# Preparing the next batch's operands in another order in a cross-attention kernel

## The chip, the cores and the metric

The kernel runs on one core of one Trainium2 chip. Its time is the device time of one execution in microseconds, the median of several runs. A core has five engines that each work through a queue of their own in program order: TensorE (PE), VectorE (DVE), ScalarE (ACT), GpSimd (POOL) and SyncE (SP, which issues DMAs here). They wait for each other by semaphores only.

## The reference

For each of 16 batches: x is 112 x 320, the context 375 x 512, of which the last 4 rows are the "ip" rows and the first 371 the text. There are 20 heads of 16 channels.

```python
q = heads(x @ W_q); k_t = heads(text @ W_k); v_t = heads(text @ W_v)
probs_t = softmax(q k_t^T / 4)                       # 112 x 371 per head
text_out = probs_t v_t
qsem = l2norm(probs_t text)                          # 112 x 512 per head
sem  = qsem · l2norm(ip)                             # 112 x 4
probs_ip = softmax(q k_ip^T / 4 + 0.5 * sem) * mask
out = (text_out + probs_ip v_ip) @ W_out + b_out + x
```

The kernel never forms `probs_t text`. It uses the Gram matrix G = text text^T (371 x 371): the squared norm of a row p of `probs_t text` is the quadratic form p G p^T, and its products with the ip rows are four more columns beside the values.

## The kernel before, in words

**Numbers.** Each float32 operand is split into a high and a low float16 part, and products are made as hi·hi + hi·lo + lo·hi. ScalarE writes the high parts out of PSUM, VectorE the low parts (value minus high part).

**Heads and steps.** The outer loop runs over 16 batches, the inner one over 20 heads; one pass of the inner loop is a step (`body` in each engine's program). In step h TensorE issues, in this order: `scores(h+3)` (one matmul, L535), `transposes(h+1)` of the probabilities (three float32 transposes, L543), in some steps one part of `finish` of the batch before, `products(h)` (p times G, L561 and L562, and p times the values, L569 and L571), and then half of a piece of the next batch's preparation (`make`). VectorE in step h: `minimum(h+3)` (L892), `probs_lo(h+1)` (`pT_lo`, L897), the low part of a piece (`make_lo`), a part of `finish`, and the quadratic form `quadratic(h)` (L907). ScalarE: `probs_hi(h+1)` (L734), `make_hi`, `exps(h+3)`, `halve(h+1)` (L740). GpSimd: `duals(h+1)` (L397: the low half of the probabilities, SBUF to SBUF), and small things.

**Pieces.** The next batch's operands come in ten pieces, which share two PSUM banks by turns (`ps_prep[k % 2]`). Piece 0 is Q, 1 to 3 are K, three are value blocks (V: 125 context rows times W_v, with 12 matmuls of 320 columns) and three are row blocks of the Gram matrix (G). Only the upper triangle of G is made: block 0 has 375 columns, block 1 250, block 2 125. So gram block 0 is the longest piece and block 2 the shortest. Block 2's piece also transposes the three upper blocks (L510) to fill the lower triangle, so it needs the high parts of blocks 0 and 1. `MAKE_STEP` makes piece k in steps 2k-1 and 2k, half each; `TAKE_STEP` evicts it to SBUF in step 2k+1 (L695 to L717 on ScalarE, L855 to L886 on VectorE). Evicting a V piece is one instruction on each engine (L716, L884). Evicting a G piece is three on ScalarE (L708, L710, L711) and four on VectorE (L871, L873, L874, L880; the profile shows them under their helpers' lines, L832 and L835).

**The end of a batch.** The ip softmax of the batch before is a chain of 13 small VectorE instructions (`soft`, numbers 0 to 12). `SOFT_AT` says in which step and at which of three places they are issued: place 0 is ahead of `probs_lo`, place 1 behind the eviction, place 2 behind `quadratic`. Between numbers 9 and 10 ScalarE takes an exponential, in step `EXP_STEP`, as its last work of the step. Number 12 is `fprob` (L968); TensorE transposes it in `finish(0)` (L594) in step 12. The four parts of `finish` use the pieces' banks, in steps 12, 14, 16 and 18; each waits until all pieces evicted so far are out of their banks:

```python
            def finish(f, k, made):
                bank = ps_prep[(k + 1) % 2]
                pe.wait_ge(s_prep_lo, made)          # made: all pieces up to h // 2 - 1
                reached(pe, s_fin_ev, NF * f.n + k)
                if k == 0:
                    pe.wait_ge(s_soft, SOFT * (f.n + 1))
```

The last batch prepares nothing; its `soft` and `finish` are one step later. The start-up makes the pieces of batch 0 one after the other in three banks, with the same order of pieces.

Of the kernel before, what the change touches and what calls it, by code (L numbers as in the profile page):

```python
# [15 lines left out]
H = 20  # L16
# [18 lines left out]


NM = 10
PIECE_Q, PIECES_K, PIECES_V, PIECES_G = 0, (1, 2, 3), (5, 7, 9), (4, 6, 8)
PIECE_TURN_G = PIECES_G[-1]
TURNED_G = 160  # L40
G_DIAG = 384
# [12 lines left out]
LAST_FINISH_STEP = {13: 0, 15: 1, 17: 2, 19: 3}  # L54


VALS_STEP, POW_STEPS, EXP_STEP = 0, (3, 4, 5, 6), 9

SOFT_AT = {(2, 0): 0, (2, 1): 1, (2, 2): 2, (3, 0): 3,
           (7, 2): 4, (8, 0): 5, (8, 1): 6, (8, 2): 7, (9, 0): 8, (9, 1): 9,  # L60
           (10, 1): 10, (10, 2): 11, (11, 0): 12}
SOFT_LATER = 1
SOFT = len(SOFT_AT)
SOFT_NORMS, SOFT_ARGS = 4, 10
# [9 lines left out]
def channels(j):  # L74
    return P if j < CC - 1 else CR
# [15 lines left out]
def build(nc, x, x_t, ctx_t, ip, ip_t, mask, w_q, w_k, w_v, w_k_ip, w_v_ip, w_out, b_out, out):  # L91
    scratch = nc.dram_tensor("v_ip_scratch", (B * NIP, C), F32, kind="Internal").ap()
    stack = ExitStack()
    with stack:
# [126 lines left out]
        def reached(eng, s, value):  # L221

            if not (isinstance(value, int) and value <= 0):
                eng.wait_ge(s, value)
# [233 lines left out]
        def _(pe):  # L458
# [12 lines left out]
            def make(a, k, banks=ps_prep, half0=0, half1=2, at=0):  # L471

                bank = banks[k % len(banks)]
                text = (text_hi[a.odd], text_lo[a.odd])
                part = range(half0 * EC // 2, half1 * EC // 2)
                if half0 == 0:
                    reached(pe, s_prep_lo, NM * a.n + k + 1 - len(banks))
                    reached(pe, s_fin_ev, NF * (a.n - 2) + sum(step <= at for step in FINISH_STEP))
                if k == PIECE_Q:
                    pe.wait_ge(s_split_pool, len(POOL_PIECES) * (a.n + 1))  # L480
                if k == PIECES_K[0]:
                    pe.wait_ge(s_split_lo, len(DVE_PIECES) * (a.n + 1))
                if k == PIECE_TURN_G and half0 == 0:
                    pe.wait_ge(s_prep_hi, NM * a.n + PIECES_G[1] + 1)
                if k in PIECES_K:
                    j = k - PIECES_K[0]
                    m = channels(j)
                    if j < CC - 1:
                        last = split3(bank[:, 0:TX], lambda h_, e: w[h_][:, e, 0, j * P:(j + 1) * P],
                                      lambda h_, e: text[h_][:, e, 0:TX], EC, part)  # L490
                    else:
                        if isinstance(a.n, int) and a.n == 0:
                            pe.wait_ge(s_wk_last, 2)
                        for e in part:
                            nc.tensor.matmul(bank[:, 0:TX], wk_last[:, e, :, :].rearrange("p a c -> p (a c)"), text[0][:, e, 0:TX],  # L495
                                             start=(e == 0), stop=(e == EC - 1), skip_group_check=True)
                            last = nc.tensor.matmul(bank[:, 0:TX], wk_last[:, e, :, :].rearrange("p a c -> p (a c)"), text[1][:, e, 0:TX],  # L497
                                                    start=False, stop=(e == EC - 1), skip_group_check=True)
                elif k == PIECE_Q:
                    for j in range(CC):  # L500
                        last = split3(bank[:, j * S:(j + 1) * S], lambda h_, c: (wq_hi, wq_lo)[h_][:, c, j * P:(j + 1) * P],
                                      lambda h_, c: (x_hi, x_lo)[h_][:, c, :], CC)
                elif k in PIECES_G:
                    i = PIECES_G.index(k)
                    m, n0 = TROWS[i], i * TC
                    hi, lo = text
                    if k == PIECE_TURN_G and half0 == 0:
                        g, blocks = gram_hi[a.odd], bank[:, TURNED_G:G_DIAG].bitcast(F16)
                        for n, (r0, c0) in enumerate(((0, 1), (0, 2), (1, 2))):
                            nc.tensor.transpose(blocks[0:TROWS[c0], n * P:n * P + TC], g[:, r0, c0 * TC:c0 * TC + TROWS[c0]], ident_16[0:TC, 0:TC])  # L510

                    for e in part:
                        nc.tensor.matmul(bank[:, G_DIAG:G_DIAG + m], hi[:, e, n0:n0 + P], lo[:, e, n0:n0 + m],  # L513
                                         start=(e == 0), stop=(e == EC - 1))
                    for e in part:
                        for term, l, r_, c in ((0, hi, hi, 0), (1, hi, lo, m), (2, lo, hi, m)):
                            last = nc.tensor.matmul(bank[:, c:T - n0], l[:, e, n0:n0 + P], r_[:, e, n0 + c:T],  # L517
                                                    start=(e == 0 and term == 0), stop=(e == EC - 1 and term == 2), skip_group_check=True)
                else:
                    i = PIECES_V.index(k)  # L520
                    m, n0 = TROWS[i], i * TC
                    last = split3(bank[:, 0:C], lambda h_, e: text[h_][:, e, n0:n0 + P],
                                  lambda h_, e: w[h_][:, e, 1, :], EC, part)
                if half1 == 2:
                    last.then_inc(s_prep, 1)
# [96 lines left out]
            last.then_inc(s_setup_pe, 1)  # L622
            pe.wait_ge(s_const, 3)
            pe.wait_ge(s_wsplit_lo, 3)
            for k in range(PIECES_G[0], PIECES_G[1] + 1):
                make(start, k, SETUP_BANKS)
            pe.wait_ge(s_w[3], 16)
            for e in range(EC):
                last = nc.tensor.matmul(ps_val[0:64, 0:C], ip_T[:, e, :], w_raw[:, e, 3, :], start=(e == 0), stop=(e == EC - 1))
            last.then_inc(s_setup_pe, 1)  # L630
            for k in range(PIECES_G[1] + 1, NM - 1):
                make(start, k, SETUP_BANKS)
            pe.wait_ge(s_ipdiag, 1)
            pe.wait_ge(s_setup_ev, 2)
# [35 lines left out]
        def _(act):  # L670
# [16 lines left out]
            def make_hi(a, k, banks=ps_prep):  # L687
# [8 lines left out]
                elif k == PIECE_Q:  # L696
                    reached(act, s_qst[1 - a.odd], 256 * (a.last().pair + 1))
                    for e in range(2):
                        last = nc.scalar.activation(q_hi[:, :, e, 0:S], bank[:, 0:CC * S].rearrange("p (c s) -> p c s", s=S),
                                                    ACT.Copy, scale=q_mask[:, e:e + 1])  # L700
                elif k in PIECES_G:
                    i = PIECES_G.index(k)
                    m, n0 = TROWS[i], i * TC
                    if i == 0:
                        reached(act, s_val, H * (a.n - 1))
                    if k == PIECE_TURN_G:
                        nc.scalar.activation(gram_hi[a.odd][:, 1, 0:TC], bank[0:TC, TURNED_G:G_DIAG].bitcast(F16)[:, 0:TC], ACT.Copy)
                    nc.scalar.activation(gram_hi[a.odd][0:m, i, n0:TX], bank[0:m, 0:TX - n0], ACT.Copy, scale=G_DOWN)  # L708
                    if i < NT - 1:
                        nc.scalar.activation(gram_2hi[0:m, i, n0 + m:TX], bank[0:m, m:TX - n0], ACT.Copy, scale=2 * G_DOWN)  # L710
                    last = nc.scalar.activation(val[a.odd][0:m, i, :, DH + 1:VW],  # L711
                                                bank[0:m, TX - n0:T - n0].unsqueeze(1).to_broadcast([m, H, NIP]), ACT.Copy, scale=G_DOWN)
                else:
                    i = PIECES_V.index(k)
                    m = TROWS[i]
                    last = nc.scalar.activation(val[a.odd][0:m, i, :, 0:DH], bank[0:m, 0:C].rearrange("p (h d) -> p h d", d=DH),  # L716
                                                ACT.Copy, scale=1.0 / W_UP)  # L717
                last.then_inc(s_prep_hi, 1)
# [61 lines left out]
            split_weight(w_hi[:, :, 1, :], w_raw[:, :, 1, :], s_w[1], 1)  # L780
            for k in range(NX):
                split_hi(Batch(1, 1, 0), k)
            for k in range(PIECES_G[0], NM - 1):
                make_hi(start, k, SETUP_BANKS)
            exps(start, 0)
            exps(start, 1)
# [43 lines left out]
        def _(dve):  # L830
# [16 lines left out]
            def make_lo(a, k, banks=ps_prep):  # L847
# [15 lines left out]
                        last = low_part(q_lo[:, :, e, 0:S], bank[:, 0:CC * S].rearrange("p (c s) -> p c s", s=S),  # L863
                                        q_mask[:, e:e + 1], q_hi[:, :, e, 0:S])
                elif k in PIECES_G:
                    i = PIECES_G.index(k)
                    m, n0 = TROWS[i], i * TC
                    if i == 0:
                        reached(dve, s_val, H * (a.n - 1))
                    g, gl, v = gram_hi[a.odd], gram_lo[a.odd], val[a.odd]  # L870
                    low_part(gl[0:m, i, n0:n0 + m], bank[0:m, 0:m], G_DOWN, g[0:m, i, n0:n0 + m]).then_inc(s_part_lo, 1)  # L871
                    if i < NT - 1:
# [8 lines left out]
                else:  # L881
                    i = PIECES_V.index(k)
                    m = TROWS[i]
                    last = low_part(val[a.odd][0:m, i, :, VW:VW + DH], bank[0:m, 0:C].rearrange("p (h d) -> p h d", d=DH),  # L884
                                    1.0 / W_UP, val[a.odd][0:m, i, :, 0:DH])
                last.then_inc(s_prep_lo, 1)  # L886
# [141 lines left out]
                                           op0=ALU.mult, op1=ALU.add, accum_out=ip_norm[:, 0:1]).then_inc(s_chain, 1)  # L1028
            dve.wait_ge(s_chain, 2)
            nc.vector.tensor_scalar(ip_norm[:, 1:2], ip_norm[:, 0:1], EPS * EPS, None, ALU.max).then_inc(s_ipsq, 1)  # L1030
            for k in range(PIECES_G[0], PIECES_G[0] + 2):
                make_lo(start, k, SETUP_BANKS)
            dve.wait_ge(s_pool_set, 2)

# [2 lines left out]
            nc.vector.tensor_scalar(ip_diag[:, :], ident[0:64, 0:64], ip_norm[:, 3:4], None, ALU.mult).then_inc(s_ipdiag, 1)  # L1037
            for k in range(NX):
                split_lo(Batch(1, 1, 0), k)
            for k in range(PIECES_G[0] + 2, NM - 1):  # L1040
                make_lo(start, k, SETUP_BANKS)
            dve.wait_ge(s_setup_pe, 2)
            nc.vector.tensor_copy(vip_rows[:, :], ps_val[0:64, 0:C]).then_inc(s_setup_ev, 1)
# [72 lines left out]
```

## Time and profile before

| | us |
|---|---|
| Median of three runs | 788.32 (787.84 to 790.66) |
| The profiled execution | 787.84 |
| its span, first to last instruction | 786.0 |
| TensorE busy, of the span | 749.9 |
| VectorE busy | 661.2 |
| ScalarE busy | 584.0 |
| GpSimd busy | 446.7 |

The profile shows one execution. "Busy" is the time in which an engine had at least one instruction in flight. Matmuls overlap each other, so the distance from one start to the next says more than the length of one. In the rows, times are microseconds from the start of the span.

### The profile page before, as it was taken

The page shows a single profiled execution, that of the slowest core. Times are in us where ns is not written, and L with a number is a line of the kernel's source. Part 1 is how long each engine was busy: PE and PEld are TensorE (multiplying, and loading weights), DVE is VectorE, ACT ScalarE, POOL GpSimd, SP SyncE. Part 2 cuts the span into 40 slices and gives each one's busy share as a digit, 9 for nine tenths or more (in the row PEclk, how much of TensorE's full clock was granted, in tenths as well). Part 3 has the DMA queues.
Part 4 walks back from the last instruction along what each step waited for, and adds up shares of the span by engine and source line. Part 5 has one row for each costly group of instructions (what it writes and reads, how often), then busy time and mean ns, then how long its engine had stood idle before and what let it go on. Part 6 is the DMA issues. An engine that isn't in the chain of part 4 may idle for free.

```text
span 786.0 us, 23798 instructions
## 1 busy us (share of the span) xinstructions
PE 749.9 (95%) x7730; PEld 588.4 (75%) x7730; DVE 661.2 (84%) x1960; ACT 584.0 (74%) x1702; POOL 446.7 (57%) x558
## 2 busy tenths in 40 slices
PE   3889999999999999999999999999999999999983
PEld 2668778787877878787787878778787777878661
DVE  5878898988989898898989889898998989889883
ACT  4378787877878787787878778787877878777770
POOL 4135574656647465664746566474656647464762
PEclk9999999999999999999999999999999999999995
DMA  9323222221412223140222314022231402021000
GB/s 268 92 55 72 79 68 62 61 79 44 103 27 66 65 59 81 42 106 24 68 65 58 81 40 108 23 67 66 55 84 41 106 21 69 21 54 41 9 2 15
DMA packets 71465, 50.02 MB, mean 64 GB/s; under 512 B 16640, under 2 KB 71280, under 8 KB 71344
## 3 DMA queue, kind: packets, MB, share of 16 engines
q1 hardware_dynamic: 68416, 45.14, 22.3%
q10 hardware_dynamic: 2928, 3.36, 1.4%
q8 instruction: 65, 1.06, 0.6%
q14 instruction: 56, 0.46, 0.2%
HBM read 20.80 MB, written 2.38 MB: 29 GB/s over the span
## 4 chain that ended last, share of the span: by engine, by line
PE 91%; issue 2%; DVE 2%; POOL 2%; ACT 1%; DMA 1%; SPq 0%; POOLq 0%; DVEq 0%; ACTq 0%
PE ps_prep L465 22%; PE ps_gram L561 19%; PE ps_pT L543 13%; PE ps_gram L562 12%; PE ps_score L535 6%; PE ps_prep L517 5%; PE ps_val L569 2%; PE ps_val L571 2%; PE ps_prep L513 1%; PE ps_prep L495 1%; PE ps_prep L597 1%; PE ps_prep L497 1%; PE ps_gram L465 1%; DMA xt_sb<-in_x_t 1%; POOL dual L397 1%
## 5 line engine op out<-in xcount | busy, mean ns | idle before, releaser
L397 POOL TENSOR_TENSOR dual<-prob 112x371 f32<-112x371 f32 x320 | 282.9, 884 | 306.6 <-ACT prob L740 287.4
L561 PE MATMUL ps_gram<-gram_hi,pT_hi 125*128 125x371 f16 (+1 forms) x960 | 303.9, 320 | 0.0
L562 PE MATMUL ps_gram<-gram_lo,pT_hi 125*128 125x371 f16 (+2 forms) x960 | 255.9, 267 | 0.0
L734 ACT ACTIVATE pT_hi<-ps_pT 125x336 f16<-125x336 f32 x320 | 144.6, 452 | 143.4 <-PE ps_pT L543 140.0
L724 ACT ACTIVATE prob<-ps_score,low 112x371 f32<-112x371 f32 x320 | 183.9, 575 | 16.5 <-DVE low L892 10.6
L892 DVE TENSOR_REDUCE low<-ps_score 112x1 f32<-112x371 f32 x320 | 171.2, 535 | 28.6 <-PE ps_score L535 24.8
L897 DVE TENSOR_TENSOR pT_lo<-ps_pT,pT_hi 125x336 f16<-125x336 f32 x320 | 160.0, 500 | 38.1 <-ACT pT_hi L734 34.0
L907 DVE CUSTOM_DVE_ANT_0 quad_junk<-ps_gram,dual 112x371 f32<-112x371 f32 x320 | 171.1, 535 | 12.4 <-PE ps_gram L562 6.0
L740 ACT ACTIVATE prob<-prob 112x371 f16<-112x371 f32 x320 | 168.9, 528 | 0.0
L569 PE MATMUL ps_val<-val,pT_hi 125*128 125x42 f16 (+1 forms) x960 | 166.9, 182 | 0.0
L543 PE MATMUL ps_pT<-ident,prob 112*125 112x112 f32 x960 | 157.0, 272 | 6.4 <-DVE pT_lo L897 3.8
L543 PEld LDWEIGHTS ps_pT<-ident,prob 112*125 112x125 f32 x960 | 142.8, 188 | 26.3 <-issue 9.5
L571 PE MATMUL ps_val<-val,pT_lo 125*128 125x21 f16 (+1 forms) x960 | 157.5, 172 | 0.0
L569 PEld LDWEIGHTS ps_val<-val,pT_hi 125*128 125x128 f16 (+1 forms) x960 | 90.1, 96 | 55.3
L571 PEld LDWEIGHTS ps_val<-val,pT_lo 125*128 125x128 f16 (+1 forms) x960 | 90.0, 97 | 19.8
L535 PE MATMUL ps_score<-k_st,q_st 128*128 128x375 f16 x320 | 103.0, 322 | 0.7 <-DVE val L832 0.7
L561 PEld LDWEIGHTS ps_gram<-gram_hi,pT_hi 125*128 125x128 f16 (+1 forms) x960 | 95.8, 100 | 5.4
L562 PEld LDWEIGHTS ps_gram<-gram_lo,pT_hi 125*128 125x128 f16 (+1 forms) x960 | 93.0, 97 | 5.3 <-issue 2.6
L407 POOL TENSOR_TENSOR nrm<-nrm,minus_half 112x5 f32<-112x5 f32 x64 | 75.0, 1173 | 1.2 <-DVE nrm L920 0.9
L728 ACT ACTIVATE ip_score<-ps_score 112x4 f32<-112x4 f32 x320 | 57.1, 178 | 0.0
L465 PE MATMUL ps_prep<-w_hi,text_lo 128*128 128x320 f16 x184 | 54.9, 298 | 0.0
L465 PE MATMUL ps_prep<-w_lo,text_hi 128*128 128x320 f16 x184 | 54.9, 298 | 0.0
(183 smaller groups left out, 1373.8 us busy)
## 6 DMA issues: line engine op xcount, KB each, us to landing
ctx_sb<-in_ctx_t SPq DMA_DIRECT2D x15, 750.0 KB, 4.5
k_st<-k_hi SPq DMA_DIRECT2D x64, 70.3 KB, 2.1
k_st<-k_lo SPq DMA_DIRECT2D x62, 70.3 KB, 2.1
q_st<-q_hi SPq DMA_DIRECT2D x64, 48.0 KB, 2.0
k_st<-k_hi SPq DMA_DIRECT2D x64, 46.9 KB, 2.0
k_st<-k_lo SPq DMA_DIRECT2D x62, 46.9 KB, 2.0
q_st<-q_lo SPq DMA_DIRECT2D x60, 48.0 KB, 2.0
x_sb<-in_x SPq DMA_DIRECT2D x16, 140.0 KB, 2.4
```

Source lines behind the costliest of these rows:

```text
L397: nc.gpsimd.tensor_tensor(dual[:, h % 2, :], prob[:, h % 4, 0:TX], prob_16[:, h % 2, :], ALU.subtract).then_inc(s_dual, 1)
L465: last = nc.tensor.matmul(dst, parts_l(a, c), parts_r(b_, c), start=(n == 0), stop=(n == total - 1))
L543: last = nc.tensor.transpose(ps_pT[0:TC, i * S:(i + 1) * S], prob[:, h % 4, i * TC:(i + 1) * TC], ident[0:S, 0:S])
L561: nc.tensor.matmul(ps_gram[h % 2][:, 0:TX], hi, gh[0:TROWS[i], i, :], start=(i == 0), stop=False, skip_group_check=True)
L562: last = nc.tensor.matmul(ps_gram[h % 2][:, i * TC:TX], hi, gl[0:TROWS[i], i, i * TC:TX], start=False, stop=(i == NT - 1), skip_group_chec ...
L569: nc.tensor.matmul(ps_val[:, o:o + 2 * VW], pT_hi[0:r, h % 2, i, :], v[0:r, i, h, :], start=(i == 0), stop=False, skip_group_check=True)
L571: last = nc.tensor.matmul(ps_val[:, o:o + VW], pT_lo[0:r, h % 2, i, :], v[0:r, i, h, 0:VW], start=False, stop=(i == NT - 1), skip_group_ch ...
L724: nc.scalar.activation(prob[:, h % 4, 0:TX], ps_score[h % 2][0:S, 0:TX], ACT.Exp, bias=low[:, h % 4:h % 4 + 1], scale=-1.0).then_inc(s_pro ...
L740: nc.scalar.activation(prob_16[:, h % 2, :], prob[:, h % 4, 0:TX], ACT.Copy, scale=0.5).then_inc(s_prob_16, 1)
L892: nc.vector.tensor_reduce(low[:, h % 4:h % 4 + 1], ps_score[h % 2][0:S, 0:TX], AX.X, ALU.min).then_inc(s_low, 1)
L897: nc.vector.tensor_tensor(pT_lo[:, h % 2, :, 0:S], ps_pT[0:TC, 0:NT * S].rearrange("p (c s) -> p c s", s=S), pT_hi[:, h % 2, :, 0:S], ALU. ...
L907: nc.vector.tensor_tensor_reduce(out=quad_junk[:, h % 2, :], in0=ps_gram[h % 2][0:S, 0:TX], in1=dual[:, h % 2, :], scale=1.0, scalar=0.0, ...
```

## The change

The pieces' numbers are dealt out anew. Before, V and G alternated: 4 = G block 0, 5 = V 0, 6 = G block 1, 7 = V 1, 8 = G block 2, 9 = V 2. After: 4 = V 0, 5 = V 1, 6 = G block 0, 7 = G block 1, 8 = G block 2, 9 = V 2. The tables of steps stay, so each piece moves with its number, on TensorE, ScalarE and VectorE. The wait that protects `val` and the Gram buffers is put on the first V piece, again piece 4. Softmax instructions 4 to 12 and the exponential get other steps and places. The start-up follows the new order. No instruction is added or removed.

```diff
-PIECE_Q, PIECES_K, PIECES_V, PIECES_G = 0, (1, 2, 3), (5, 7, 9), (4, 6, 8)
+PIECE_Q, PIECES_K, PIECES_V, PIECES_G = 0, (1, 2, 3), (4, 5, 9), (6, 7, 8)
...
-VALS_STEP, POW_STEPS, EXP_STEP = 0, (3, 4, 5, 6), 9
+VALS_STEP, POW_STEPS, EXP_STEP = 0, (3, 4, 5, 6), 10

 SOFT_AT = {(2, 0): 0, (2, 1): 1, (2, 2): 2, (3, 0): 3,
-           (7, 2): 4, (8, 0): 5, (8, 1): 6, (8, 2): 7, (9, 0): 8, (9, 1): 9,
-           (10, 1): 10, (10, 2): 11, (11, 0): 12}
+           (8, 0): 4, (8, 1): 5, (8, 2): 6, (9, 0): 7, (9, 1): 8, (9, 2): 9,
+           (11, 0): 10, (11, 1): 11, (11, 2): 12}
...
@@ TensorE, start-up
-            for k in range(PIECES_G[0], PIECES_G[1] + 1):
+            for k in range(PIECES_V[0], PIECES_G[1]):
                 make(start, k, SETUP_BANKS)
...
-            for k in range(PIECES_G[1] + 1, NM - 1):
+            for k in PIECES_G[1:]:
                 make(start, k, SETUP_BANKS)
@@ ScalarE and VectorE, eviction of a G piece
-                    i = PIECES_G.index(k)
+                    i = k - PIECES_G[0]
                     m, n0 = TROWS[i], i * TC
-                    if i == 0:
-                        reached(act, s_val, H * (a.n - 1))
@@ and of a V piece
                     i = PIECES_V.index(k)
                     m = TROWS[i]
+                    if i == 0:
+                        reached(act, s_val, H * (a.n - 1))
@@ VectorE, start-up
-            for k in range(PIECES_G[0], PIECES_G[0] + 2):
+            for k in PIECES_V[:2]:
                 make_lo(start, k, SETUP_BANKS)
...
-            for k in range(PIECES_G[0] + 2, NM - 1):
+            for k in PIECES_G:
                 make_lo(start, k, SETUP_BANKS)
```

## Rows read from the trace of the kernel before

**Rows 1.** The page, busy us, share of the span and instructions of each engine.

```profile
PE 749.9 (95%) x7730; PEld 588.4 (75%) x7730; DVE 661.2 (84%) x1960; ACT 584.0 (74%) x1702; POOL 446.7 (57%) x558
```

**Rows 2.** The page, chain that ended last, shares by engine.

```profile
PE 91%; issue 2%; DVE 2%; POOL 2%; ACT 1%; DMA 1%; SPq 0%; POOLq 0%; DVEq 0%; ACTq 0%
```

**Rows 3.** Timeline of TensorE, batch 6, steps 8 to 15: start, length, instruction.

```profile
334.98 0.32 PE L535 MATMUL ps_score<-k_st,q_st 128*128 128x375 f16 x1
...
337.25 0.32 PE L535 MATMUL ps_score<-k_st,q_st 128*128 128x375 f16 x1
...
341.72 0.32 PE L535 MATMUL ps_score<-k_st,q_st 128*128 128x375 f16 x1
...
343.71 0.32 PE L535 MATMUL ps_score<-k_st,q_st 128*128 128x375 f16 x1
...
344.35 0.26 PE L594 MATMUL ps_prep<-ident,fprob 112*80 112x112 f32 x1
...
345.94 0.32 PE L535 MATMUL ps_score<-k_st,q_st 128*128 128x375 f16 x1
...
348.17 0.32 PE L535 MATMUL ps_score<-k_st,q_st 128*128 128x375 f16 x1
...
348.64 0.48 PE L597 MATMUL ps_prep<-vip_diag,fprob_T 80*112 80x320 f32 x1
...
350.99 0.32 PE L535 MATMUL ps_score<-k_st,q_st 128*128 128x375 f16 x1
...
352.41 0.36 PE L510 MATMUL ps_prep<-ident,gram_hi 125*125 125x125 f16 x3
```

**Rows 4.** Timeline of VectorE and GpSimd in step 11 of batch 6.

```profile
342.20 0.27 DVE L965 RECIPROCAL fmax<-fmax 112x20 f32<-112x20 f32 x1
342.39 0.48 DVE L892 TENSOR_REDUCE low<-ps_score 112x1 f32<-112x371 f32 x1
342.79 0.61 DVE L968 SCALAR_TENSOR_TENSOR fprob<-fexp,mask_sb,fmax 112x80 f32<-112x80 f32 x1
343.32 0.49 DVE L897 TENSOR_TENSOR pT_lo<-ps_pT,pT_hi 125x336 f16<-125x336 f32 x1
343.74 0.48 DVE L832 SCALAR_TENSOR_TENSOR val<-ps_prep,val 125x320 f16<-125x320 f32 x1
...
344.60 0.08 DVE L907 DVE_READ_ACCUMULATOR2_ANT quad<- 112x1 f32 x1
...
342.42 0.84 POOL L397 TENSOR_TENSOR dual<-prob 112x371 f32<-112x371 f32 x1 [1.02 <-ACT prob L740]
...
344.20 0.89 POOL L397 TENSOR_TENSOR dual<-prob 112x371 f32<-112x371 f32 x1
```

**Rows 5.** Timeline of VectorE and ScalarE in step 13, eviction of gram block 1.

```profile
347.10 0.51 DVE L897 TENSOR_TENSOR pT_lo<-ps_pT,pT_hi 125x336 f16<-125x336 f32 x1 [0.25 <-ACT pT_hi L734]
...
348.27 0.28 DVE L835 SCALAR_TENSOR_TENSOR gram_lo<-ps_prep,gram_lo 125x125 f16<-125x125 f32 x1
...
347.37 0.32 ACT L711 ACTIVATE val<-ps_prep 125x80 f16<-125x80 f32 x1
```

**Rows 6.** Timeline of VectorE in step 9, end of the eviction of gram block 0.

```profile
339.93 0.28 DVE L835 SCALAR_TENSOR_TENSOR gram_lo<-ps_prep,gram_lo 125x125 f16<-125x125 f32 x1
```

**Rows 7.** All runs of line 968: shortest, median and longest in ns.

```profile
L968 DVE SCALAR_TENSOR_TENSOR fprob<-fexp,mask_sb,fmax x16: 302/608/608, 113.0 to 775.2; 112x80 f32<-112x80 f32 x16
```

**Rows 8.** Timeline of the start-up: what follows gram block 1, and its eviction's end.

```profile
31.78 0.48 PE L629 MATMUL ps_val<-w_raw,ip_T 128*64 128x320 f32 x1
...
32.31 0.32 ACT L711 ACTIVATE val<-ps_prep 125x80 f16<-125x80 f32 x1
```

**Rows 9.** Stretches of the start-up: length, busy us by engine, PEclk (granted clock), DMA.

```profile
22.90:25.50 2.60, 0.07 (x2) 0.00 (x0) 2.51 (x6) 1.39 (x4) 1.36 (x2) 1.00 0.09 22
26.00:29.30 3.30, 3.30 (x15) 2.04 (x14) 2.82 (x7) 0.51 (x2) 0.24 (x1) 0.50 0.22 49
38.90:42.10 3.20, 1.57 (x10) 0.89 (x9) 2.06 (x5) 2.23 (x7) 0.53 (x1) 1.00 0.84 290
```

More of the change, by code:

```diff
@@ L701, in make_hi @@
                 elif k in PIECES_G:
-                    i = PIECES_G.index(k)
+                    i = k - PIECES_G[0]
                     m, n0 = TROWS[i], i * TC
-                    if i == 0:
-                        reached(act, s_val, H * (a.n - 1))
                     if k == PIECE_TURN_G:
@@ L782, in _ @@
                 split_hi(Batch(1, 1, 0), k)
-            for k in range(PIECES_G[0], NM - 1):
+            for k in range(PIECES_V[0], NM - 1):
                 make_hi(start, k, SETUP_BANKS)
@@ L865, in make_lo @@
                 elif k in PIECES_G:
-                    i = PIECES_G.index(k)
+                    i = k - PIECES_G[0]
                     m, n0 = TROWS[i], i * TC
-                    if i == 0:
-                        reached(dve, s_val, H * (a.n - 1))
                     g, gl, v = gram_hi[a.odd], gram_lo[a.odd], val[a.odd]
@@ L883, in make_lo @@
                     m = TROWS[i]
+                    if i == 0:
+                        reached(dve, s_val, H * (a.n - 1))
                     last = low_part(val[a.odd][0:m, i, :, VW:VW + DH], bank[0:m, 0:C].rearrange("p (h d) -> p h d", d=DH),
```

## The prediction

> **What bounds the kernel now.** I read the page's busy times first: the span is 786.0 us and TensorE is busy for 95% of it, VectorE for 84% [rows 1]. The chain that ended last is 91% TensorE, with 2% each for VectorE, GpSimd and bare issue [rows 2]. So nearly the whole time is one in-order queue, TensorE's, and a change that moves no matrix work can cost time only by making that queue wait. The place to look is therefore the timeline of one batch, step by step. I took batch 6, whose step 8 starts at 334.98; a step starts where its score matmul (L535) starts. The batches repeat closely: `fprob` (L968) took 608 ns in the median of its 16 runs and 608 ns at most [rows 7].
>
> From [rows 3], steps last as follows. Step 8 (a half of gram piece 0): 337.25 - 334.98 = 2.27 us. Step 11 (a half of gram piece 1): 343.71 - 341.72 = 1.99. The difference, 0.28, is the size of the two halves. `finish(1)` (L597) starts 348.64 - 348.17 = 0.47 after its step starts; `finish(0)` (L594) starts 344.35 - 343.71 = 0.64 after its own. So step 12 already holds a wait of 0.17 us, for `pT_lo` of head 12, which VectorE starts at 343.32 [rows 4] where it normally starts 1.16 after the step's start (347.10 - 345.94, [rows 3, 5]).
>
> **Part 1: TensorE's own work.** It is permuted, not changed. Steps 7 and 8 make a value piece, 9 and 10 another, 11 and 12 gram piece 0, 13 and 14 gram piece 1. Step 11 gets 2.27 us instead of 1.99, step 13 gets 1.99 in exchange. Sum over a batch: 0. VectorE's and ScalarE's evictions are permuted likewise: also 0 by themselves. No DMA is issued elsewhere: context, x and restack transfers hang on pieces 0 to 3 and on the splits, which don't move.
>
> **Part 2: relief.** At step 9 VectorE now evicts a value piece (one instruction) instead of gram piece 0 (four), and the softmax instructions 10 to 12 start later, so it enters step 11 without its present lag. The wait of 0.17 in step 12 goes: -0.17 per batch. It could be 0 if the lag stays. What is late next in that step is `finish(0)` itself.
>
> **Part 3: finish(0) in step 12 waits for softmax instruction 12.** That instruction (`fprob`, L968) stood first in VectorE's step 11; now it stands behind `pT_lo`, the value eviction, instruction 11 and the quadratic form. Forward from step 11's start, at VectorE's own pace: `pT_lo` at 1.16; the eviction 0.42 later (343.74 - 343.32), at 1.58; eviction and quadratic form together take 0.86 (344.60 - 343.74); instruction 11 takes 0.19 (342.39 - 342.20) [rows 4]. So `fprob` starts at 2.63. GpSimd's `dual` of the next head starts at 344.20 - 341.72 = 2.48 [rows 3, 4]. Today's `fprob` shows what that means: it started 0.37 after such a `dual` (342.42) and ended at 343.40, 0.98 after the `dual`'s start, taking 608 ns; the one run with an idle GpSimd took 302 [rows 4, 7]. Take off its own 0.30: it is let in 0.68 after the `dual`'s start. Hence it ends at 2.48 + 0.68 + 0.30 = 3.46; a release of TensorE by VectorE takes 0.09 (348.55 to 348.64, [rows 3, 5]). TensorE is there at 2.27 + 0.47 = 2.74. Wait: 3.55 - 2.74 = **0.81 us**. If `fprob` gets in before the `dual` (its margin is only 0.15): 2.63 + 0.30 + 0.09 - 2.74 = 0.28. Upper bound, with a latency of 0.15: 0.87. I take 0.81, as the start times say that `dual` is first.
>
> The Trainium skill (SBUF — State Buffer, "Who interferes with whom") says that a VectorE instruction with two SBUF inputs and a GpSimd one that reads SBUF exclude each other, the first one for its whole length. The trace agrees in kind, 608 against 302 ns. By the `dual`'s full recorded length (0.84, [rows 4]) the wait would be 0.16 longer, 2.2 us over 14 batches; I go by the measured 0.68, as the recorded GpSimd lengths are rough.
>
> **Part 4: finish(1) in step 14 waits for piece 6.** `finish` waits until the piece evicted one step earlier is free of its bank. Piece 6 was gram piece 1 (its last eviction instruction, L835, ends at 348.27 + 0.28 - 345.94 = 2.61 after step 13's start [rows 3, 5]); with 0.09 of latency that is exactly when TensorE arrives now, 348.64. Now it is gram piece 0, whose L835 ends at 339.93 + 0.28 - 337.25 = 2.96 after its step's start [rows 3, 6], bound by ScalarE's three wider copies ahead of it. And TensorE arrives earlier, as step 13 is short: 1.99 + 0.47 = 2.46. Wait: 2.96 + 0.09 - 2.46 = **0.59 us**. Lower bound, if gram piece 0 were evicted as fast as piece 1: 2.70 - 2.46 = 0.24. Upper, with a lag of 0.1 at the step's start: 0.7.
>
> **Part 5: the turned blocks in step 15 wait for gram piece 1.** Piece 8 transposes `gram_hi` of rows 0 and 1, and waits for ScalarE's eviction of gram piece 1. That used to be done two steps earlier; now it happens in step 15 itself. TensorE reaches the transposes at 352.41 - 350.99 = 1.42 after the step's start [rows 3]. ScalarE finishes gram piece 1 at 347.37 + 0.32 - 345.94 = 1.75 after its step's start [rows 3, 5]. Wait: 1.75 + 0.09 - 1.42 = **0.42 us**. Bounds 0.33 (no latency) and 0.5. This one needs no `finish`, so it also falls in batch 0. `finish(2)` in step 16 then comes after all of piece 7's eviction (ends at 2.61; TensorE is there at 1.99 + 0.42 + 0.47 = 2.88): 0. The waits don't absorb each other, since VectorE and ScalarE re-start each step from TensorE's scores and transposes.
>
> **Part 6: the start-up.** There the turned blocks follow the piece before at once. That piece will be gram piece 1, whose eviction ended at 32.31 + 0.32 = 32.63, 0.85 after TensorE left it at 31.78 [rows 8]. With latency **0.94 us**, and the first minima, exponentials and products stand behind it. Bounds 0 (hidden) and 1.2.
>
> **Part 7: the last batch** makes no pieces, but `fprob` moves from the first to the third place of step 12 there as well, before `finish(0)` in step 13. By Part 3's pieces (0.42 + 0.19 + 0.44 + 0.30 = 1.35 behind the start of `pT_lo`, the 0.44 being 0.86 - 0.42; TensorE comes some 0.9 behind it, by a wait of 0.5 for `pT_lo` and its three transposes) I estimate **0.5 us**, bounds 0 and 0.8. The other new places of softmax instructions 4 to 9 and of ScalarE's exponential lie in steps 8 to 10, where VectorE now has one eviction instruction in place of four: 0.
>
> **Sum.** A full batch: 0.81 + 0.59 + 0.42 - 0.17 = 1.65 us; 14 batches (1 to 14) have it: 23.1. Batch 0: 0.42. Start-up 0.94, last batch 0.5. Total 25.0 us on the profiled execution's 787.84 (span 786.0), the lowest of the three runs, whose median is 788.32: **813 us**. All low bounds: 14 x (0.28 + 0.24 + 0.33 - 0.17) + 0.33 = 9.9, so 798. All high: 14 x (0.87 + 0.7 + 0.5) + 0.5 + 1.2 + 0.8 = 31.5, so 819.
>
> **Rivals.**
> - *fprob goes ahead of the dual.* Same three waits, but the first is 0.28: 0.53 x 14 = 7.4 us less, 805.5. For it: the margin is 0.15. Against: both start times come from undisturbed steps. Chance 0.2.
> - *One wait absorbs the others.* If the pause in one step let the helpers run ahead, only the turned blocks, whose input is made within the step, would stay: 14 x (0.42 - 0.17) + 0.42 + 0.94 = 4.9, so 793. Against: VectorE can't run ahead of scores that don't exist. Chance 0.08.
> - *The clock falls.* After 2.60 us with TensorE all but idle its granted clock was 0.50, 1.2 GHz, for the next 3.3 us; yet it stayed at 1.00, 2.4 GHz, through 3.20 us in which it was busy for 1.57 [rows 9]. The new pauses are 0.4 to 0.8 us between busy steps, far milder. One such fall costs 3.3 / 2 = 1.65 us; in 15 batches 25 us more, 838. Chance 0.05. The Trainium skill (TensorE: Matmul & The Clock Gate, Part 1) says that low activity throttles the clock and activity releases it; the trace agrees.
> - *The other side: no slower.* The evening out wins if ScalarE's part of gram piece 0 overlaps so well that steps 14 and 15 have no wait and `fprob` is in time; it decides if that eviction ends before 2.37 in its step instead of 2.96. Then only the relief is left: 787.84 - 14 x 0.17 = 785.5. For it: VectorE's load becomes more even. Against: every number of Parts 3 to 5. Chance 0.04.
>
> **How the numbers follow.** The forecast has 0.6, the rivals 0.2, 0.08, 0.05 and 0.04, the rest lies between. The first rival and the forecast share one range, 800 to 820, which holds them with nearly all of their bounds. Half a per cent, 3.9 us, is what a measurement here can tell from no change. Slower by more than that: 0.95; within it 0.04; faster 0.01.
>
> **What would show it.** In the profile after: a TensorE idle row at L594 of about 0.8 us released by L968, one at L597 of 0.6 released by L835, one at L510 of 0.4 released by ScalarE's L711, 14, 14 and 15 times; a batch period longer by 1.65 us; `pT_lo` 1.16 after step 11's start; the granted clock unchanged. A period that doesn't grow, or growth elsewhere than steps 12, 14 and 15, would make the prediction wrong.

## The result, and the profile after

| | before | after |
|---|---|---|
| Median, us | 788.08 (787.55 to 790.66) | 814.98 (814.54 to 815.56) |
| Profiled execution | 787.84 | 813.73 |
| its span | 786.0 | 811.9 |
| Batch period (14 alike) | 45.97 | 47.72 |

The changed kernel is slower: the ratio is 1.0335, with a 95% interval of 1.0311 to 1.0359. The forecast was 813 us. The changed kernel's profiled execution, 813.73, is a fifth one beside the four whose median this is.

First the page of the kernel after: busy times, and the chain that ended last. They answer to [rows 1] and [rows 2].

```profile
PE 754.8 (93%) x7730; PEld 590.8 (73%) x7730; DVE 673.1 (83%) x1960; ACT 582.2 (72%) x1702; POOL 444.8 (55%) x558
...
PE 79%; DVE 7%; issue 6%; ACT 5%; POOL 1%; DMA 1%; SPq 0%; POOLq 0%; ACTq 0%; DVEq 0%
```

The instruction counts are the same. The chain, which was 91% TensorE, now goes through VectorE for 7% and ScalarE for 5% of the span: TensorE waits for them. For whom exactly, the list of waits says (engine, line waited at, releaser: us in total, times, longest):

```profile
PE ps_prep L594 <- DVE fprob L968: 18.2, 16, 8.5
...
PE ps_prep L597 <- DVE gram_lo L835: 5.6, 14, 0.4
...
PE ps_prep L510 <- ACT val L709: 5.0, 15, 0.3
...
PE ps_gram L510 <- ACT val L709: 0.9, 1, 0.9
```

These are the forecast's three places, with its three releasers. The counts are its 14, 14 and 15, and in addition the last batch and the tail at L594 and the start-up at L510 (`ps_gram`). Of the 18.2 us at L594, 8.5 is the wait in the tail, which the kernel before has too. (L709 is the old L711; the diff moved it by two lines.) The idle times understate the waits: a matmul is recorded as lasting beyond the start of the next one (353.86 + 0.32 against 354.02, below), so part of each wait counts as busy. Starts are the better measure. TensorE in steps 12 to 15 of batch 6:

```profile
353.86 0.32 PE L535 MATMUL ps_score<-k_st,q_st 128*128 128x375 f16 x1
354.02 0.48 PE L543 MATMUL ps_pT<-ident,prob 112*125 112x112 f32 x3
355.18 0.27 PE L594 MATMUL ps_prep<-ident,fprob 112*80 112x112 f32 x1 [0.68 <-DVE fprob L968]
...
357.10 0.32 PE L535 MATMUL ps_score<-k_st,q_st 128*128 128x375 f16 x1
...
359.06 0.32 PE L535 MATMUL ps_score<-k_st,q_st 128*128 128x375 f16 x1
...
360.11 0.79 PE L597 MATMUL ps_prep<-vip_diag,fprob_T 80*112 80x320 f32 x2 [0.41 <-DVE gram_lo L835]
...
362.22 0.32 PE L535 MATMUL ps_score<-k_st,q_st 128*128 128x375 f16 x1
...
364.12 0.35 PE L510 MATMUL ps_prep<-ident,gram_hi 125*125 125x125 f16 x3 [0.33 <-ACT val L709]
```

L594 starts 355.18 - 353.86 = 1.32 after its step, where 0.47 is undisturbed: a wait of 0.85. L597 starts 1.05 after its step: 0.58. L510 starts 1.90 after its step where it started 1.42 after it [rows 3]: 0.48. The transposes of step 12 start 0.16 after the score, as in steps without a wait: the old wait of 0.17 is gone.

VectorE and GpSimd in the same stretch, against [rows 4]:

```profile
353.17 0.48 DVE L832 SCALAR_TENSOR_TENSOR val<-ps_prep,val 125x320 f16<-125x320 f32 x1
353.56 0.27 DVE L965 RECIPROCAL fmax<-fmax 112x20 f32<-112x20 f32 x1
353.75 0.48 DVE L907 CUSTOM_DVE_ANT_0 quad_junk<-ps_gram,dual 112x371 f32<-112x371 f32 x1
354.15 0.08 DVE L907 DVE_READ_ACCUMULATOR2_ANT quad<- 112x1 f32 x1
354.15 0.87 DVE L968 SCALAR_TENSOR_TENSOR fprob<-fexp,mask_sb,fmax 112x80 f32<-112x80 f32 x1
...
354.04 0.89 POOL L397 TENSOR_TENSOR dual<-prob 112x371 f32<-112x371 f32 x1 [0.56 <-ACT prob L740]
```

`fprob` starts 0.11 behind the `dual` and ends at 355.02, which is 0.98 after the `dual`'s start, to the hundredth what it was in the kernel before.

Where the time went, by steps. A step's length is the distance between two score matmuls, here the median of ten batches; steps that aren't named have the same length, within 0.01, in both:

| step | 7 + 8 | 11 | 12 | 13 | 14 | 15 | sum |
|---|---|---|---|---|---|---|---|
| before | 4.56 | 1.99 | 2.23 | 2.23 | 2.82 | 1.94 | |
| after | 4.46 | 2.28 | 3.23 | 1.96 | 3.16 | 2.41 | |
| difference | -0.10 | +0.29 | +1.00 | -0.27 | +0.34 | +0.47 | +1.73 |

The matrix work that moved cancels (longer halves in 11 and 12, shorter ones in 7, 8, 13 and 14). What is left is 0.85 + 0.58 + 0.48 - 0.17 = 1.74 of the period's 1.75.

That is a full batch. The start-up, batch 0 and the last batch have other sums. The score matmuls (L535) that begin them started at these times in the two profiled executions:

| | step 0 of batch 0 | of batch 1 | of batch 15 | end |
|---|---|---|---|---|
| before | 41.26 | 86.28 | 729.75 | 786.03 |
| after | 41.51 | 87.47 | 755.50 | 811.92 |

| grown by | start-up | batch 0 | batches 1 to 14 | last batch | sum |
|---|---|---|---|---|---|
| forecast | 0.94 | 0.42 | 23.1 | 0.5 | 25.0 |
| measured | 0.25 | 0.94 | 24.56 | 0.14 | 25.89 |

### The profile page after: what moved, and what is told of

It is laid out like the page before. It is cut to its first block, busy times and chain, and to the rows that moved or that the text cites. A ratio compares the mean times of both kernels' runs of the same rounds, so it can differ in the third digit from the quotient of the medians.

```text
span 811.9 us, 23798 instructions
## 1 busy us (share of the span) xinstructions
PE 754.8 (93%) x7730; PEld 590.8 (73%) x7730; DVE 673.1 (83%) x1960; ACT 582.2 (72%) x1702; POOL 444.8 (55%) x558
## 4 chain that ended last, share of the span: by engine, by line
PE 79%; DVE 7%; issue 6%; ACT 5%; POOL 1%; DMA 1%; SPq 0%; POOLq 0%; ACTq 0%; DVEq 0%
PE ps_prep L465 21%; PE ps_gram L561 16%; PE ps_pT L543 11%; PE ps_gram L562 10%; PE ps_score L535 5%; PE ps_prep L517 3%; PE ps_val L569 2%; ACT gram_hi L706 2%; PE ps_val L571 2%; PE ps_prep L597 2%; DVE fprob L968 1%; PE ps_prep L495 1%; PE ps_prep L497 1%; ACT val L709 1%; PE ps_gram L465 1%
## 5 line engine op out<-in xcount | busy, mean ns | idle before, releaser
L561 PE MATMUL ps_gram<-gram_hi,pT_hi 125*128 125x371 f16 (+1 forms) x960 | 303.8, 320 | 0.0
L535 PE MATMUL ps_score<-k_st,q_st 128*128 128x375 f16 x320 | 103.0, 322 | 0.7 <-DVE val L832 0.7
L561 PEld LDWEIGHTS ps_gram<-gram_hi,pT_hi 125*128 125x128 f16 (+1 forms) x960 | 95.7, 100 | 5.5
```

Source lines behind the costliest of these rows:

```text
L561: nc.tensor.matmul(ps_gram[h % 2][:, 0:TX], hi, gh[0:TROWS[i], i, :], start=(i == 0), stop=False, skip_group_check=True)
```

## The experiments

The theory: three separate waits, each set by something that TensorE's next instruction needs and that is now made later. The rival: the helpers (VectorE, ScalarE and GpSimd) are simply too busy, and a wait that is taken away at one place comes back at the next. Each run was compared with the kernel before on the same chip; the ratios are to that one.

**Each half of the change alone.** The places of the softmax instructions, on the old order of pieces:

```diff
-VALS_STEP, POW_STEPS, EXP_STEP = 0, (3, 4, 5, 6), 9
+VALS_STEP, POW_STEPS, EXP_STEP = 0, (3, 4, 5, 6), 10
-           (7, 2): 4, (8, 0): 5, (8, 1): 6, (8, 2): 7, (9, 0): 8, (9, 1): 9,
-           (10, 1): 10, (10, 2): 11, (11, 0): 12}
+           (8, 0): 4, (8, 1): 5, (8, 2): 6, (9, 0): 7, (9, 1): 8, (9, 2): 9,
+           (11, 0): 10, (11, 1): 11, (11, 2): 12}
```

> The kernel before, with only the new places of the softmax instructions and of the exponential; pieces in the old order. Separate waits: gram piece 0 is then evicted in step 9 with three softmax instructions around it, so VectorE reaches `pT_lo` of head 11 some 0.5 us too late for TensorE in step 11, and `fprob` comes last in a step 11 that lasts only 1.99 us: a wait of 0.7 to 1.2 us at `finish(0)`. Together 1.1 to 1.6 us in each of 14 batches, so 803 to 810, most likely 806; no wait at `finish(1)` nor at the turned blocks. A fixed wait for `fprob` alone (0.84 + 0.28 for the shorter step - 0.17) would give 788 + 13 = 801.

Measured: 811.75 us, ratio 1.0308 (1.0291 to 1.0325), a period of 47.64. The mechanism is there, and it is dearer than I had it, just above the expected range. The timeline of steps 10 and 11 shows what was left out of the sum (VectorE, GpSimd, then TensorE):

```profile
347.85 0.77 DVE L960 TENSOR_TENSOR fused<-fused,fmax 112x80 f32<-112x80 f32 x1
348.54 0.53 DVE L892 TENSOR_REDUCE low<-ps_score 112x1 f32<-112x371 f32 x1
348.99 0.49 DVE L897 TENSOR_TENSOR pT_lo<-ps_pT,pT_hi 125x336 f16<-125x336 f32 x1
...
347.69 0.83 POOL L397 TENSOR_TENSOR dual<-prob 112x371 f32<-112x371 f32 x1 [1.34 <-ACT prob L740]
...
348.85 0.32 PE L535 MATMUL ps_score<-k_st,q_st 128*128 128x375 f16 x1
349.63 0.33 PE L543 MATMUL ps_pT<-ident,prob 112*125 112x112 f32 x1 [0.46 <-DVE pT_lo L897]
```

Softmax instruction 9 (L960), 0.23 us long when alone, falls behind a `dual` and takes 0.77; `pT_lo` is late by that, and the transposes start 0.78 instead of 0.16 after the score. `finish(0)` then starts 1.62 after step 12, a wait of 1.15.

The new order of pieces with the old softmax places:

> The changed kernel with the old places of the softmax instructions and the exponential; pieces in the new order. Separate waits: no wait at L594, 0.57 at L597, 0.48 at L510 (these two as the changed kernel shows them), the old 0.17 in step 12 gone: 14 x (0.57 + 0.48 - 0.17) + 0.48 = 12.8, plus some 0.5 in the start-up and batch 0: 801. If the waits absorbed one another (VectorE is simply too busy, and any relief at one place comes back at another), it would stay near 815.

Measured: 802.2 us, ratio 1.0189 (1.0171 to 1.0207), period 46.87. L594 starts 0.47 after its step (no wait), L597 1.04, L510 1.90: exactly two of the three waits. The total is 1 us above the expected 801, because in its profile batch 0 grew by 1.12 (46.13 against 45.01) and the start-up by 1.14; both are taken up below. So order of pieces alone costs 0.91 us a batch, softmax places alone 1.68, both together only 1.75. They overlap. With both, the wait of 0.62 in step 11 is gone and the one at `finish(0)` is 0.85 instead of 1.15; against that, the relief of 0.17, which each half brings alone, comes only once. The likely reason is that the new order takes the heavy eviction out of step 9 and makes step 11 longer; no run separates these two.

**What holds fprob for 0.87 us.** It can be the `dual` that GpSimd runs at that moment (the port theory of the expectation: both engines read SBUF, and one shuts the other out), or something of its own. This kernel leaves out most of one `dual`:

```diff
-                nc.gpsimd.tensor_tensor(dual[:, h % 2, :], prob[:, h % 4, 0:TX], prob_16[:, h % 2, :], ALU.subtract).then_inc(s_dual, 1)
+                w = 16 if h == 12 else TX
+                nc.gpsimd.tensor_tensor(dual[:, h % 2, 0:w], prob[:, h % 4, 0:w], prob_16[:, h % 2, 0:w], ALU.subtract).then_inc(s_dual, 1)
```

> The changed kernel, but GpSimd makes only 16 of the 371 columns of head 12's `dual` (that head's quadratic form is left incomplete). Port theory: `fprob` starts 0.06 to 0.15 us behind this `dual` and stands still until it lets go; with a short `dual` it takes 0.30 instead of 0.87 us, the wait at `finish(0)` falls from 0.84 to 0.27 us, 14 x 0.57 = 8.0 less: 807. If `fprob` is slow for another reason (its operands, its place behind the quadratic form) nothing changes: 815, length of L968 still 0.87.

Measured: 807.32 us, ratio 1.025 (1.0235 to 1.0265). Its row of all runs (shortest, median, longest in ns; the diff adds a line) and the two instructions in batch 6:

```profile
L969 DVE SCALAR_TENSOR_TENSOR fprob<-fexp,mask_sb,fmax x16: 295/297/939, 117.0 to 795.1; 112x80 f32<-112x80 f32 x16
```

```profile
352.74 0.30 DVE L969 SCALAR_TENSOR_TENSOR fprob<-fexp,mask_sb,fmax 112x80 f32<-112x80 f32 x1
...
352.63 0.21 POOL L398 TENSOR_TENSOR dual<-prob 112x16 f32<-112x16 f32 x1 [0.56 <-ACT prob L741]
```

Same operands, same place, same start relative to the step; only the other engine's instruction is short, and `fprob` takes 0.30. `finish(0)` starts 0.74 after its step: a wait of 0.27, as expected. The collision with the `dual` is worth 0.57 us a batch, a third of the whole loss. (The 939 ns are the last batch's `fprob`, which runs in step 12 beside another head's full `dual`.)

**finish(1), and finish(0) with it, behind the products.**

```diff
+                    behind = prepare and finish_step.get(h) in (1,)
-                    if finishing and h in finish_step:
+                    if finishing and h in finish_step and not behind:
                         finish(b.last(), finish_step[h], NM * (b.n + 1) + (h // 2 if prepare else 0))
                     products(b, h)
+                    if finishing and behind:
+                        finish(b.last(), finish_step[h], NM * (b.n + 1) + h // 2)
```

> The changed kernel, with `finish(1)` issued behind the products of step 14 instead of ahead of them. Separate waits: gram piece 0 is out of its bank long before (0.95 us of products hide 0.57 of wait): 14 x 0.57 = 8.0 less, 807, and the waits at L594 (0.84) and L510 (0.48) stay as they are. Absorption: the quadratic form of step 14 now comes later and VectorE enters step 15 late, so that L510 or L601 wait longer by the same; 812 to 815.

Measured: 805.7 us, ratio 1.023 (1.0214 to 1.0245), period 47.14, so 0.57 less than the changed kernel. Step 14 goes from 3.16 to 2.58, all others stay. L594 and L510 keep their waits. With `(0, 1)` in place of `(1,)`:

> The changed kernel, with `finish(0)` and `finish(1)` issued behind the products of their steps. Separate waits: both waits (0.84 and 0.57) are hidden by 0.95 us of products: 14 x 1.41 = 19.7 less, 795, and L510 keeps its 0.48. Absorption: more than 800.

Measured: 795.44 us, ratio 1.0092 (1.0076 to 1.0108), period 46.29. Steps 12 and 14 go to 2.39 and 2.58; L510 still starts 1.90 after its step. These waits are separate: what is taken away does not come back.

**The turned blocks one step later.** Here the theory itself foresees that a wait comes back:

```diff
-                if k == PIECE_TURN_G and half0 == 0:
-                    pe.wait_ge(s_prep_hi, NM * a.n + PIECES_G[1] + 1)
...
                                                     start=(e == 0 and term == 0), stop=(e == EC - 1 and term == 2), skip_group_check=True)
+                    if k == PIECE_TURN_G and half1 == 2:
+                        pe.wait_ge(s_prep_hi, NM * a.n + PIECES_G[1] + 1)
+                        g, blocks = gram_hi[a.odd], bank[:, TURNED_G:G_DIAG].bitcast(F16)
+                        for n, (r0, c0) in enumerate(((0, 1), (0, 2), (1, 2))):
+                            last = nc.tensor.transpose(blocks[0:TROWS[c0], n * P:n * P + TC], g[:, r0, c0 * TC:c0 * TC + TROWS[c0]], ident_16[0:TC, 0:TC])
```

> The changed kernel, with the three turned blocks (L510) and their wait at the end of piece 8, in step 16, instead of at its start in step 15. By the chain of readiness: TensorE loses the wait of 0.48 at L510, but then reaches `finish(2)` 2.2 us after step 15's start, and that one needs all of gram piece 1 out of its bank, which is so at 2.61 + 0.1 to 0.15: it now waits 0.5 there. Nothing is gained: 814 to 816, with the wait at L601 instead of L510. If the turned blocks alone were the cause, 15 x 0.48 = 7.2 less: 807.8.

Measured: 814.37 us, ratio 1.0335 (1.0317 to 1.0354), period 47.76 against 47.72. TensorE in steps 15 and 16 (L533 is the score, L599 `finish(2)`, L516 the transposes):

```profile
362.22 0.32 PE L533 MATMUL ps_score<-k_st,q_st 128*128 128x375 f16 x1
...
363.96 0.32 PE L533 MATMUL ps_score<-k_st,q_st 128*128 128x375 f16 x1
364.12 0.48 PE L541 MATMUL ps_pT<-ident,prob 112*125 112x112 f32 x3
364.89 0.51 PE L599 MATMUL ps_prep<-ident,attn 112*128 112x112 f32 x3 [0.29 <-DVE gram_lo L833]
...
366.50 0.36 PE L516 MATMUL ps_prep<-ident,gram_hi 125*125 125x125 f16 x3
```

Step 15 falls from 2.41 to 1.74, and step 16 grows from 2.02 to 2.73: `finish(2)` now starts 0.93 after its step and waits for VectorE's eviction of the same piece, gram block 1. One cause, an eviction made a step too late, stands behind both places, and the wait moves between them.

**All repairs together,** `finish(0)`, `(1)` and `(2)` behind the products and the turned blocks late:

> The changed kernel with `finish(0)`, `finish(1)` and `finish(2)` behind the products of their steps and the turned blocks at the end of piece 8. If the three new waits are the whole cause, nothing of the loss is left in the batches: 814.7 - 14 x (0.84 + 0.57 + 0.48) - 0.48 = 788, within 0.5% of the kernel before, perhaps 2 us less since the old wait of 0.17 in step 12 is gone too. If something else also grew (total helper load, the order of the pieces by itself), 792 or more.

Measured: 790.2 us, ratio 1.0017 (1.0004 to 1.0031), period 46.05, so 1.67 of the 1.75 is gone and 0.08 is left. That is 2 us above the expected 788 and below the 792 of the alternative. Had all three waits gone and nothing come back, the period would lie below the old one by the relief of 0.17. It lies above it because a new wait stands in step 18, 3.64 instead of 3.46: `finish(3)` starts 0.62 after its step instead of 0.47. In the timeline ScalarE's `attn_out`, released 0.9 us later in step 16, pushes the exponential, the copy of `pT_hi` and so `pT_lo` and the eviction of piece 8 in step 17. Here the rival has its share: of some 1.9 us of waits taken away, 0.18 came back at another place.

**Better than both?** Two old waits remained in the kernel before. First the one of 0.17:

```diff
-           (10, 1): 10, (10, 2): 11, (11, 0): 12}
+           (10, 1): 10, (10, 2): 11, (11, 1): 12}
```

> The kernel before, with `fprob` (softmax number 12) one place later in step 11, behind `pT_lo` and the eviction instead of ahead of them. By the timeline `pT_lo` of head 12 then starts when its input is there (1.16 instead of 1.60 us into the step) and the wait of 0.17 us in step 12 goes, while `fprob`, starting at 1.98, is done at 2.3, ahead of both the next `dual` (2.48) and `finish(0)` (2.46): 14 x 0.17 = 2.4 us less, 785.7. If it collides with the `dual` instead, `finish(0)` waits some 1 us: 800.

Measured: 787.47 us, ratio 0.9986 (0.997 to 1.0002), period 45.93, 0.03 less instead of 0.17. `fprob` missed the `dual`, but not GpSimd's next instruction, the split of a context block:

```profile
343.00 0.43 DVE L968 SCALAR_TENSOR_TENSOR fprob<-fexp,mask_sb,fmax 112x80 f32<-112x80 f32 x1
...
342.49 0.84 POOL L388 TENSOR_TENSOR text_lo<-ctx_sb,text_hi 128x375 f16<-128x375 f32 x1
...
343.57 0.27 PE L594 MATMUL ps_prep<-ident,fprob 112*80 112x112 f32 x1
```

It ends at 343.43, where its own 0.30 would have taken it to 343.30; `finish(0)` starts 0.14 behind it, 0.12 late. A new wait took most of the place of the old one, and I had not looked at that row.

Then the wait of 0.29 at the start of each batch:

```diff
-FINISH_STEP = {12: 0, 14: 1, 16: 2, 18: 3}
+FINISH_STEP = {12: 0, 14: 1, 16: 2, 19: 3}
```

> The kernel before, with `finish(3)` in step 19 instead of 18. Step 19 makes no piece and lasts only 1.42 us, too short for the way from its transposes over ScalarE and VectorE to the next ones, so step 0 begins with a wait of 0.29 us. With 1.22 us of `finish(3)` in step 19 this wait goes: 14 x 0.29 = 4.1 us less, 784. If the output's way (eviction and ScalarE's store, now both in step 19) holds up ScalarE's first work of the next batch, nothing or a loss.

Measured: **783.56 us, ratio 0.9938 (0.9916 to 0.9961)**. The period is 45.65, 0.31 less. Step 0 falls from 3.05 to 2.75. The transposes of step 0 in the kernel before, and in this one:

```profile
362.06 0.32 PE L535 MATMUL ps_score<-k_st,q_st 128*128 128x375 f16 x1
362.45 0.33 PE L543 MATMUL ps_pT<-ident,prob 112*125 112x112 f32 x1
```

```profile
360.67 0.32 PE L535 MATMUL ps_score<-k_st,q_st 128*128 128x375 f16 x1
360.82 0.48 PE L543 MATMUL ps_pT<-ident,prob 112*125 112x112 f32 x3
```

They started 0.39 after the score and now start 0.15 after it. The other 0.06 of the step's 0.30 lies between the transposes: the row of the kernel before holds only the first of the three, as the second started 0.17 behind it, where the distance is 0.10 without a wait. Both edits:

> The kernel before, with both: `fprob` one place later and `finish(3)` in step 19. If the two waits are separate, the gains add up: 14 x 0.46 = 6.5 us less, 781.6; this would beat both kernels.

Measured: 783.48 us, ratio 0.9939 (0.9918 to 0.9959), the same as the second alone, as the first brings next to nothing.

Last, whether the new order of pieces is any worse by itself, once nobody waits for it:

> The changed kernel with its three new waits repaired as above, and also `finish(3)` in step 19. The last repair left a batch period of 46.05 us: in it `finish(3)` waits 0.15 us in step 18 for the eviction of piece 8, and step 0 still begins with its old wait of 0.29. Both should go: 45.6, so 14 x 0.31 = 4.3 us less than the kernel before, 783.5, the same as the old order of pieces with `finish(3)` in step 19 (period 45.65). If the new order of pieces were itself the better or the worse one, the period would differ from 45.65 by more than 0.1.

Measured: 783.69 us, ratio 0.9938 (0.9921 to 0.9955), period 45.56 against 45.65. The two orders are worth the same, though not in kernels that are alike otherwise: this one has three parts of `finish` behind the products and no longer the old wait of 0.17, which the other still has. It is the waits that made the change slow, not the order.

## Why the prediction was right

The mechanism was right: three waits, at the places, with the releasers and nearly the sizes that Parts 3 to 5 give. That the total came so close, 25.0 forecast against 25.9 on the profiled execution, is in part luck. The terms missed by +1.5 (the 14 batches), +0.5 (batch 0), -0.7 (start-up) and -0.4 (last batch), and these misses nearly cancel.

- *Part 1, matrix work permuted: 0.* The steps' table sums to the waits within 0.01.
- *Part 2, relief: -0.17.* Gone, as the transposes' start shows.
- *Part 3, finish(0): 0.81.* Measured 0.85. `fprob` started 2.57 after step 11 (353.86 - 351.58 = 2.28 for the step, and 0.29 into the next) where 2.63 was forecast, still behind the `dual`, which started at 2.46. The transpose started 0.16 behind it (355.02 to 355.18), not 0.09. The rival in which `fprob` goes first did not happen; the short `dual` shows what it would have brought.
- *Part 4, finish(1): 0.59.* Measured 0.58.
- *Part 5, turned blocks: 0.42.* Measured 0.48; the latency is 0.14 (363.65 + 0.33 = 363.98, below, to 364.12) rather than 0.09.

```profile
363.65 0.33 ACT L709 ACTIVATE val<-ps_prep 125x80 f16<-125x80 f32 x1
```

- *The 0.09.* It was read where there is no wait: in the kernel before L597 starts 0.47 after its step, as it does undisturbed, and the end of L835 only happens to lie 0.09 ahead. Where TensorE does wait for it, L597 starts 0.06 behind L835's end (359.77 + 0.28 = 360.05 to 360.11), less than the 0.14 to 0.16 of the two places above. A latency has to be read at an instruction that waits.

```profile
359.77 0.28 DVE L835 SCALAR_TENSOR_TENSOR gram_lo<-ps_prep,gram_lo 125x125 f16<-125x125 f32 x1
```

- *"finish(2): 0".* Right, but only because TensorE was already held up at the turned blocks; the experiment that took that wait away found it at `finish(2)`. The sentence "the waits don't absorb each other" was true for steps 12, 14 and 15, not for 15 and 16.
- *Batch 0: 0.42.* Measured 0.94, over its upper bound of 0.5. With no batch to finish, step 14 lasts only 1.96 there, and VectorE and ScalarE come out of gram block 0's long eviction late. TensorE in step 15 of batch 0, in the kernel after:

```profile
76.96 0.32 PE L535 MATMUL ps_score<-k_st,q_st 128*128 128x375 f16 x1
77.45 0.55 PE L543 MATMUL ps_pT<-ident,prob 112*125 112x112 f32 x3 [0.18 <-DVE pT_lo L897]
...
79.27 0.35 PE L510 MATMUL ps_prep<-ident,gram_hi 125*125 125x125 f16 x3 [0.33 <-ACT val L709]
```

The transposes start 0.49 after the score instead of 0.16, and the turned blocks 2.31 instead of 1.42. So the sentence that the helpers re-start each step from TensorE's scores and transposes does not hold behind a step this short.

- *Part 6, start-up: 0.94.* Between the two profiled executions the first products start only 0.25 later (42.40 against 42.15). The wait is there all the same: the kernel before lost about as much, and more, to a fall of the clock that the kernel after did not have. Compare profiles by order of pieces and by clock, from the matmul behind TensorE's long start-up pause (25.57 us before, 26.39 us after) to the first product (L561), in us:

| clock between 25 and 31 us | old order | new order | difference |
|---|---|---|---|
| 1.00 throughout | 14.90 (softmax places alone; `fprob` one place later) | 16.00 (the kernel after) | 1.10 |
| 0.50 for 3.4 us | 16.58 (the kernel before; `finish(3)` in step 19; both edits) | 17.68 (short `dual`), 17.70 (`finish(0)` and `(1)` behind) | 1.1 |

(Two more profiles of the new order had a second fall within the stretch, and three make the turned blocks later; they are left out.) The wait costs 1.1 us, inside the bounds of 0 and 1.2, and one fall of the clock 16.58 - 14.90 = 1.68. In the profile after, that fall was missing and the stretch began 0.82 later (26.39 against 25.57): 1.10 - 1.68 + 0.82 = 0.24.

- *Part 7, last batch: 0.5.* Measured 0.14. Its `finish(0)` starts 1.22 after its step where it started 0.95 after it, and steps 11 to 13 are longer, but step 10 is 0.76 shorter (2.08 instead of 2.84): its transposes start 0.74 instead of 1.50 after the score, as the softmax instructions there moved too. The prediction put the other new places at 0.
- *The clock:* the granted clock was 1.00 from 17.9 us to 796.1 us in the execution after. Pauses of 0.5 to 0.85 us did not lower it. The trace agrees with the forecast's reading.

The Trainium skill's rule on the shared port (SBUF — State Buffer, "Who interferes with whom") passed a direct test: with the `dual` cut short `fprob` took 0.30 us. The page has the loser blocked for the other's whole instruction. The trace shows `fprob` ending 0.98 after the `dual`'s start, both before and after, so it was let in at 0.68 if its own part is the 0.30 that it takes alone, while the `dual` is recorded as 0.84 to 0.89. The measured 0.68 is the number to plan with.

## What to carry to other kernels

When one in-order engine is the bottleneck, a reordering that adds no work is priced by arrival against readiness: for each wait that the moved instructions stand behind or ahead of, take the step-relative time at which the bottleneck arrives and the one at which its input is ready, and sum only the positive differences. Look one wait further than the one you take away, since the same late producer may hold the next instruction. And before you move a small two-input SBUF instruction on VectorE, look at what GpSimd runs at that moment: here it turned 0.3 us into 0.87.

## What the runs showed of the hardware

The start-up of nearly the same program differs between executions by more than most effects here. The first products started between 40.8 and 44.2 us in the thirteen profiles; 1.1 us of that is the order of pieces. In three of them (the kernel after among them), TensorE's clock stayed at 2.4 GHz throughout the start-up, in the others it fell once or twice for 3.4 us. Two such stretches of one execution (the kernel with the new order of pieces alone; length, busy us by engine, then PEclk, which is 0.50, that is 1.2 GHz):

```profile
25.80:29.10 3.30, 3.30 (x14) 1.82 (x13) 3.02 (x7) 0.23 (x1) 0.00 (x0) 0.50 0.31 70
42.90:46.20 3.30, 3.30 (x24) 2.57 (x25) 1.71 (x3) 1.86 (x4) 0.69 (x1) 0.50 0.09 11
```

In the kernel before, TensorE had been idle for 2.6 us when the clock fell [rows 9]; in the kernel after it was idle for 2.4 us at the same place (24.0 to 26.4) and the clock did not fall. The length of the pause does not tell the two apart: nine of the profiles have a pause of 2.40 us there, and the clock fell behind it in four and stayed in five. One fall costs 1.7 us, so a single execution's total says little about an effect of 1 us. Batch periods, which repeat to 0.01 us in the kernels before and after, are the measure to trust.
